# Vision-transformer tower with a state-space block and a switch router on one core: the first pair's front beside the tap products, and the router's arithmetic placed in the drain

## The reference, cut to what matters

```
h  = patches @ W.T + b ; h = concat(cls_tok, h)              # 64 x 197 x 192
xz = layernorm(h) @ W_in ; x_inner, z = split(xz)            # 384 and 384
x  = silu(conv4(x_inner, conv_w) + conv_b)                   # taps over tokens, 384 -> 384
B, C = split(x @ W_x) ; delta = softplus(x @ W_dt + b_dt)    # 16 states
h_t = exp(delta_t * A) * h_(t-1) + (delta_t * x_t) * B_t     # the scan, per channel and state
y  = (sum over states of h_t * C_t + D * x) * silu(z)
h  = h + layernorm(y @ W_out) * gamma + beta
probs = softmax(layernorm(h) @ switch_w + switch_b)          # 8 experts
# route = argmax, rank of a token in its expert by descending prob, keep rank < capacity
h  = h + (expert(layernorm(h)) if kept else layernorm(h)) * max(probs)
```

## Time and profile before

| | |
|---|---|
| runs shown | 2964.89, 2957.38 and 2966.27 us, median 2964.89 |
| profiled execution | 2954.76 us, its span 2953.0 us |
| busy share of the span | TensorE 84%, VectorE 77%, ScalarE 67%, GpSimd 79% |
| first convolution begins | 65.19 us into the span |
| VectorE's first scan begins | 126.29 us |
| last pair's logits taken | 2328.92 us |
| mean granted clock of TensorE | 0.938 |

### The profile page before, as it was taken

How to read it: one execution, slowest core, us unless ns; L and a number is a source line. 1 busy time by engine, 2 the same in 40 slices (tenths; PEclk the granted TensorE clock), 3 DMA queues, 4 the chain that set the end, 5 groups by cost and what they waited for, 6 DMA issues and landing times.

```text
span 2953.0 us, 37695 instructions
## 1 busy us (share of the span) xinstructions
PE 2476.0 (84%) x12595; PEld 1554.0 (53%) x12595; DVE 2284.6 (77%) x2318; ACT 1980.9 (67%) x4114; POOL 2345.2 (79%) x1322
## 2 busy tenths in 40 slices
PE   5888888888888888888888888888874379999997
PEld 3444444444444454444444444454431267888886
DVE  1399999999999999999999999999999484222222
ACT  0677787778878877788778878877785153343432
POOL 0389999999999999999999999999998324544442
PEclk8899999999999999999999999999996589999999
DMA  3444455544445544555544445544443025666652
GB/s 100 99 99 107 113 125 122 124 113 107 107 114 131 123 108 107 123 117 123 125 108 107 107 115 128 122 110 107 114 110 65 17 97 166 211 217 208 214 188 90
DMA packets 165463, 361.07 MB, mean 122 GB/s; under 512 B 18353, under 2 KB 89593, under 8 KB 157848
## 3 DMA queue, kind: packets, MB, share of 16 engines
q1 hardware_dynamic: 152504, 329.59, 44.4%
q0 software_dynamic: 12768, 29.08, 3.1%
HBM read 293.86 MB, written 69.30 MB: 123 GB/s over the span
## 4 chain that ended last, share of the span: by engine, by line
PE 42%; DVE 24%; ACT 14%; issue 9%; DMA 8%; POOL 1%; SPq 1%; DVEq 0%; another core or an unknown queue 0%; ACTq 0%; POOLq 0%
DVE arena L1441 13%; DMA arena<-in_x 8%; PE banks L1340 7%; PE banks L1004 7%; DVE arena L1430 6%; PE banks L1023 6%; ACT banks L714 5%; PE banks L1319 5%; PE banks L1072 4%; ACT arena L721 3%; PE banks L1327 3%; PE banks L1025 2%; PE banks L1084 2%; ACT L701 1%; DVE arena L1448 1%
## 5 line engine op out<-in xcount | busy, mean ns | idle before, releaser
L1441 DVE TENSOR_TENSOR_SCAN arena<-banks,arena 128x788 f32<-128x788 f32 x768 | 1342.1, 1786 | 93.8 <-ACT banks L714 60.6
L522 POOL TENSOR_TENSOR arena<-arena 128x1576 f32<-128x1576 f32 x384 | 1248.7, 3260 | 27.2 <-DVE arena L1441 27.1
L714 ACT ACTIVATE banks<-arena,neg_a 128x392 f32<-128x392 f32 x1536 | 840.4, 582 | 308.7 <-DVE arena L1441 298.9
L1430 DVE TENSOR_TENSOR arena<-arena,banks 128x1576 f32<-128x1576 f32 x320 | 568.2, 1776 | 25.8 <-PE banks L1057 25.7
L1072 PE MATMUL banks<-arena,gather_q 128*32 128x394 f32 x3072 | 355.7, 537 | 11.2 <-POOL arena L522 11.2
L1004 PE MATMUL banks<-wtok,arena 128*99 128x192 f32 x1536 | 290.0, 355 | 63.9 <-DMA arena<-in_x 59.2
L672 POOL DMA_INDIRECT out_tokens<-arena x114 | 114.9, 1008 | 256.3 <-DVE arena L1637 237.1
L1004 PEld LDWEIGHTS banks<-wtok,arena 128*99 128x99 f32 x1536 | 274.5, 183 | 77.6 <-issue 70.9
L1023 PE MATMUL banks<-arena,v_lo 128*128 128x394 f32 x768 | 308.3, 547 | 2.3 <-ACT arena L763 1.3
L1622 DVE TENSOR_TENSOR arena<-banks,arena 128x384 f32<-128x384 f32 x57 | 31.8, 557 | 353.3 <-PE banks L1340 312.3
L1041 PE MATMUL banks<-arena,wdt 128*128 128x394 f32 x576 | 213.2, 506 | 33.8 <-ACT arena L788 33.8
(11 more groups left out here) (237 smaller groups left out, 4045.1 us busy)
## 6 DMA issues: line engine op xcount, KB each, us to landing
arena<-delta_du_scratch SPq DMA_DIRECT2D x384, 394.0 KB, 10.5
arena<-in_w_pack SPq DMA_DIRECT2D x57, 1155.0 KB
delta_du_scratch<-arena SPq DMA_DIRECT2D x96, 394.0 KB, 3.2
arena<-in_x SPq DMA_DIRECT2D x32, 1176.0 KB, 11.8
rows_scratch<-arena SPq DMA_DIRECT2D x32, 297.0 KB
rows_scratch<-arena SPq DMA_DIRECT2D x32, 294.0 KB
arena<-in_b SPq DMA_DIRECT2D x57, 96.0 KB
arena<-in_conv_w SPq DMA_DIRECT2D x1, 2304.0 KB, 9.1
```

Source lines behind the costliest of these rows:

```text
L522: pool.tensor_tensor(v[:, :, :], v[:, :, :], c_rep[r][:, u % NG].unsqueeze(1).to_broadcast([P, NQ, N2]), ALU.mult).then_inc(s_mulp, 1)
L714: ins = act.activation(o, d, ACT.Exp, scale=neg_a[:, c:c + 1])
L1430: dve.tensor_tensor(hb[(UNITS * n + u) % BUFS][:, :, :], rep[m][:, :, 1, :], ps_b[:, 0:N2].unsqueeze(1).to_broadcast([P, NQ, N2]), ALU.mul ...
L1441: dve.tensor_tensor_scan(v, decay[k % 2], v, 0.0, ALU.mult, ALU.add).then_inc(s_scan, 1)
```

## The change

**Head.** SyncE loads the token bias, the token weights and the first pair's patches first, the class row behind the bias, then the tap weights, and the 17 other loads after these. TensorE multiplies the first pair's tokens ahead of the tap products, which now use banks 4 and 5, and transposes the first pair's normalised tokens ahead of the last two tap products. VectorE makes `pick` and `gather_q` before anything lands, then the first pair's embedding and statistics, then the tap copies, and `skip` and the centred `wout` behind them. New semaphores `s_wtok`, `s_bias` and `s_skip` carry the finer waits. The first pair's delta is made by VectorE (`first_delta`), ahead of `body(-1)`, and GpSimd leaves it out.

**Drain.** FIRST leaves out the last two pairs (eight columns) and its steps stand earlier on three engines.

```
-FIRST, LAST = slice(0, COLS - 4), slice(COLS - 4, COLS)
+FIRST, LAST = slice(0, COLS - 8), slice(COLS - 8, COLS)
...
@@ block.sync
+            for f in range(2):
+                sp.dma_start(tok_bias[:, f, :], tok_b.partition_broadcast(H0)).then_inc(s_bias, 16)
+            sp.dma_start(wtok[:, :, :], tok_w).then_inc(s_wtok, 16)
+            sp.dma_start(patches[:, :, :, 1:L], x[0]).then_inc(s_patch, 16)
+            sp.wait_ge(s_bias, 32)
+            sp.dma_start(tok_bias[0:1, 0, :], cls_tok).then_inc(s_clsrow, 16)
+            sp.dma_start(raw_win, w_inx).then_inc(s_taps, 16)
+            sp.dma_start(raw_taps, conv_w).then_inc(s_taps, 16)
...
@@ block.gpsimd: softplus_sum, softplus_rest, make_delta, make_du
+                if n == 0:
+                    return
@@ block.scalar: body
+                        if i == PAIRS:
+                            router_exp(FIRST, 1)
                         row_norm(i - 2, r)
-                        if i == PAIRS + 1:
-                            router_exp(FIRST, 1)
@@ block.tensor: body, and ahead of the loop
                     if -2 in on and u == 6:
+                        if i == PAIRS + 1:
+                            rank(FIRST, 1)
...
+            pe.wait_ge(s_wtok, 16)
+            pe.wait_ge(s_dve0, 1)
+            pe.wait_ge(s_pool0, POOL0)
+            for b in range(2):
+                tok(0, 0, b, True)
+            pe.wait_ge(s_taps, 32)
...
+                    if n == 2 * TAPS - 2:
+                        for b in range(2):
+                            front_t(0, 0, b, True)
...
-            rank(FIRST, 1)
@@ block.vector
+            dve.wait_ge(s_clsrow, 16)
+            for b in range(2):
+                embed(0, 0, 0, b, True)
+            front_stats(0, 0, True)
...
+            def first_delta():
+                dve.wait_ge(s_spe, 1)
+                dve.tensor_tensor(spv[:, :, :], spv[:, :, :], spe[:, :, :], ALU.add).then_inc(s_spd, 1)
+                dve.wait_ge(s_spd, 1)
+                dve.wait_ge(s_spt, 1)
+                dve.tensor_tensor(spv[:, :, :], spv[:, :, :], delta[:, :, :], ALU.subtract).then_inc(s_spc, 1)
+                dve.wait_ge(s_spc, 1)
+                dve.wait_ge(s_spl, 1)
+                dve.tensor_tensor(delta[:, :, :], spv[:, :, :], du[:, :, :], ALU.add).then_inc(s_delta, 1)
+                dve.wait_ge(s_delta, 1)
+                dve.wait_ge(s_x, 1)
+                dve.tensor_tensor(du[:, :, :], delta[:, :, :], xz[0][:, 0:MB, :], ALU.mult).then_inc(s_du, 1)
...
-                dve.wait_ge(s_lg, PAIRS - 1 if c == FIRST else PAIRS)
+                dve.wait_ge(s_lg, PAIRS - 2 if c == FIRST else PAIRS)
...
                     if -1 in on and k == 5:
+                        if i == PAIRS:
+                            shift(FIRST)
                         take_y(i - 1, o, 2)
...
                     if -2 in on and k == 19:
+                        if i == PAIRS:
+                            weigh(FIRST, 1)
+                        if i == PAIRS:
+                            choose(FIRST)
+                        if i == PAIRS + 1:
+                            ranks(FIRST, 1)
                         take_logits(i - 2, r)
-                        if i == PAIRS:
-                            shift(FIRST)
-                        if i == PAIRS + 1:
-                            weigh(FIRST, 1)
...
             for i in range(-2, PAIRS + 2):
+                if i == -1:
+                    first_delta()
                 body(i, i % 2, range(-i, PAIRS - i))
-            choose(FIRST)
-            ranks(FIRST, 1)
```

95 lines of the change are left out of this document (54 added, 41 removed).

## The result

The changed kernel took 2915.53 us (median of 4 runs, 2908.32 to 2924.99), the kernel before, beside it, 2961.14 (4 runs, 2954.69 to 2966.27). The ratio is 0.9849, with a 95% interval of 0.9813 to 0.9885: 45.6 us gained, where 55.0 had been forecast; the interval of the ratio is 34 to 55 us. The profiled execution of the change took 2908.32 us (span 2906.6; before 2953.0).

A forecast was written before the change was run, and what follows sets the result against it. VectorE and GpSimd were taken to bound the pair loop, so only its ends could gain. Head 30.5 plus drain 24.5 gave 55.0 us off the median 2964.89: 2909.9 us, range 2895 to 2924.

The forecast's parts named there:

- Head, the landing of the tokens: Opening loads: token products start near 9.2 us, low end 8.1, high end 11.5.
- the three terms: Token start in the opening: issue near 2.1, plus 6.0 for patches to land, plus 1.2 for bytes ahead.
- the 0.45 MB ahead of the patches at 365 GB/s: Opening loads: bytes still to move before the patches, priced at 1.2 us.
- Head, TensorE: Opening on TensorE: first convolution at 37.95 against 65.19, 27.2 us earlier, plus 2.8 from the higher clock.
- half a head: Rival, opening: late tokens, low clock in the first convolution, embedding holds TensorE; 7.7 us less gain, 2918; chance 0.15.
- Head, the first delta: First pair's delta moved to VectorE: passes of 1.38 us, only 0.5 us of gain passes through.
- Their 3.4 us buy nothing: Opening: delta ready 3.4 us ahead of GpSimd gains nothing, as VectorE's first product waits for the B spread.
- Drain: End of the pair loop to the expert stage: router work moved into waits saves 24.5 us, worst 21, best 25.
- the 0.8 us of add_residual: Drain, GpSimd: add_residual falls from 2.63 to 1.81 us with the shift no longer beside it.
- The contention rule that I weighed: Drain: GpSimd shares SBUF interfaces with VectorE; two small GpSimd chains of pair 31 stretch, costing 1.6 us.
- The pair loop is a block of fixed length: Pair loop, 124 to 2262 us: VectorE and GpSimd set its rate, the change leaves their work per pair alone.
- a sign of being wrong: Pair loop: longer by over 5 us would be a cause the working does not have.

The follow-up runs named there:

- e4: The change with token weights and patches issued ahead of the broadcast bias loads, SyncE's bias wait behind the tap loads: 2898.29 us, ratio 0.9838 to the kernel before.
- e8: The change with e3's threshold edit and token weights and patches ahead of the bias rows, no load waiting for another: 2892.77 us, ratio 0.9782 to the kernel before.
- e10: The change with all three edits, e8 and e9 together: 2862.93 us, ratio 0.9717 to the kernel before.
- e11: e10 with the first pair's delta back on GpSimd: 2867.80 us, ratio 0.9717 to the kernel before.
- e12: e10 with nine unread matmuls on TensorE ahead of the first pair's wx products: 2868.02 us, ratio 0.9712 to the kernel before.
- e7: The change itself, unaltered, measured again on another chip: 2904.92 us against 2955.67 for the kernel before, ratio 0.9829.
- e2: The kernel before with the change's drain only: 2927.62 us, ratio 0.9926 to the kernel before.
- e3: The change with each bisection threshold made by scalar_tensor_tensor instead of tensor_scalar: 2885.05 us, ratio 0.9781 to the kernel before.
- e9: The change with each later pair's patches issued one pair earlier, ahead of the store of the rows: 2877.95 us, ratio 0.9765 to the kernel before.
- e1: The change's opening with the drain of the kernel before: 2915.49 us against 2948.89 for the kernel before, ratio 0.9885.
- e6: The change with the first pair's delta back on GpSimd: 2900.52 us, ratio 0.9808 to the kernel before.
- e5: The kernel before with the threshold by scalar_tensor_tensor alone: 2947.85 us, ratio 0.9973 to the kernel before.

## Why the prediction was right, and where it was not

**The time.** 2910 was forecast, within 2895 to 2924; measured 2915.5. Of the 55 us, 45.6 came in the first measurement, 50.8 in the second, and 54.7 as the sum of the parts; all agree with 55 and with each other within their intervals. The 5.6 us between 2909.9 and 2915.5 are a gain 9.4 short on a kernel before that measured 3.8 us below the 2964.89 I had set in. And luck helped the profile: its loop was 7.1 us shorter than the one before, for no reason of the change's, and that hid most of the 9.0 us of the expert stage.

**Head, the landing of the tokens: wrong.** 9.2 was forecast (the three terms add up to 9.3) with 11.5 as the high end; measured 12.30, 11.60 and 11.58. The term that failed is the 0.45 MB ahead of the patches at 365 GB/s. The change's own opening (GB/s in 40 slices of 0 to 26 us) shows why:

```profile
GB/s 0 0 0 65 73 43 30 150 330 367 364 365 359 339 348 453 424 425 422 425 425 454 454 397 388 241 210 336 269 375 260 191 194 116 28 51 91 38 142 289
```

The two bias rows, 99 pieces of 768 B each, stand first and move at 30 to 73 GB/s for four slices, 2.6 us. I had priced them by their bytes. With the patches ahead of them the tokens start at 8.38 to 9.69 (e4, e8, e10, e11, e12). Whether it is the small pieces that are slow, or that all 99 read the same row, no run parts.

**Head, TensorE: right.** 16.8 us of taps behind the tokens, 0.7 for the transposes, 0.8 for the last copy, the higher clock (2.88 for 2.8): 29.06 us from the tokens' start to the first convolution in the change, 28.2 in e7, 28.75 forecast. The late tokens shifted it by 1.8 us in e7 (39.79 for 37.95); then the wx products, at the higher clock in e7 (2.23 us; 3.17 in the profile before), gave most of that back, and the first product stood at 94.2 for 93.9. Two errors cancelled there: that 94.2 meets 93.9 is luck. In the first profile they did not cancel, and it was 99.0. Of the three conditions of "half a head" only the late tokens came true.

**Head, the first delta: right.** "Their 3.4 us buy nothing": e11 says so. VectorE's passes took 1.39 us (forecast 1.38), and the product waited for the B spread.

**Drain: right to a us.** 24.1 - 0.4 was forecast; logits to one-hots fell by 23.5. Both parts fitted into the waits, with 1.6 and 1.3 us to spare (forecast 1.8 and 1.1). Of the 0.8 us of add_residual (1.81 us, as forecast) only 0.4 arrived ahead of the logits, and the shift, moved, now lies beside two of GpSimd's products with C: 7.38 us for two instead of 6.45 in the first profile (7.4 also in e2, e3, e7, e9 and e10, 6.45 in e1 with the old drain), and the last y comes 0.2 to 1.0 us later. The whole: 21.3 us measured in e2 (15 to 29 by its interval) against 24.5. The contention rule that I weighed (the Trainium skill, "GPSIMD Engine Reference", Key points) agrees with this place, where the shift's second instruction has two SBUF inputs, with 0.9 us; I had looked for it at the wrong chains.

**"The pair loop is a block of fixed length": wrong.** With the same instructions it took 2098.0 to 2116.4 us over the ten profiles up to e8 (2116.4 in e6). This is a scatter larger than most terms of the sum; e6's and e8's loops are longer than before's by more than the 5 us that I had named as a sign of being wrong. The mean also hid the best gain: rows 1 average VectorE's 94% over pairs from 66.8 us to 69.5, and in the slow pair that I looked into TensorE waits for patches and then runs at its lower clock. I had taken an engine at 94% as a sign that nothing was to be had elsewhere; e9 shows 20 us.

**The expert stage** had no term. Of the 9.0 us more of the first profile some 6 are the held threshold, which that profile paid and the kernel before's profile happened not to, and 4.6 a wait that the trace can't name. Nothing ties either to the change's edits: e1, e2 and e7 show 531 us on two other chips, and e5 has the kernel before gain 7.8 us by the same edit. And both profiles of the first measurement lost some 11 to 13 us more than those of the experiments behind the first expert output, which cancelled in their difference.

## What to carry to other kernels

Ask first whether a shortfall of the sum is clear of noise, and ablate both halves of the change before explaining it: here the halves gave the forecast, and the 9 us were within the interval. When a stage whose code did not change differs between two profiles, look for the same loss in both: here the largest one stood in both and cancelled. Compare the shortest with the longest turn of a loop: this loop had a busy engine and turns of unequal length, the slices around its first slow instruction named a late load, and issuing that earlier was worth more than the opening's last 3 us and the threshold together. In an opening, price small broadcast loads by the rate at which such loads moved and not by their bytes, and put them behind whatever the first instruction waits for.

## What the hardware showed that I had not expected

- VectorE's tensor_scalar on 114 x 4 elements, 0.23 us alone, took 3.22 to 5.09 us when it came within GpSimd's memset of 4.83 us or up to 0.3 us ahead of it, and ended with it; a scalar_tensor_tensor of the same size took 0.16 us at the same place, and tensor_reduce and tensor_tensor passed as well. The Trainium skill ("GPSIMD Engine Reference", Key points) names VectorE's two-port modes and its instructions with two SBUF inputs as what contends with GpSimd. The first would agree, but nothing here shows the mode itself; the second was not held beside this memset: the tensor_tensor of 114 x 512 has two SBUF inputs and took its usual 0.69 us.
- Two broadcasts of 74.2 KB each at the head of a queue moved at 30 to 73 GB/s, at a fifth or less of the 365 that followed.
- The same opening gave a first product anywhere from 93.9 to 99.0 us, with the same instructions and waits on TensorE. Of these 5.1 us 1.9 were there at the first convolution (41.36 and, in e9, 39.51: tokens 0.9 later, and their passes 10.95 us for 10.01), and 2.9 came in the wx and delta products behind the wait of 3.27 us (10.93 us for 8.02 to the next tokens), which ran in part at TensorE's lower clock.
